# Layer-1 attention: the sum matmuls of a head moved straight behind its last V product, additions of the exponentials in one run, and the orders around them

## The chip, the cores and the metric

The kernel runs as one program on one core of a Trainium2 chip. The metric is the time of one execution on the device in microseconds, the median of several runs. One execution is also taken by the hardware profiler; its rows are counted from the start of the profiled span. The engines are TensorE (PE, with its weight loads PEld), VectorE (DVE), ScalarE (ACT), GpSimd (POOL) and SyncE (SP), which issues the transfers.

## The reference, cut to what matters

Two transformer layers with modulated norms over x of 4 batches x 1024 tokens x 128. The change is inside the attention of the second one (layer 1): 16 heads of width 64 in each of 4 batches, 64 heads in all.

```python
xn = layer_norm(x, ln_gamma, ln_beta)
q, k, v = heads(xn @ Wq), heads(xn @ Wk), heads(xn @ Wv)
att = jnp.einsum('bhid,bhjd->bhij', q, k) / DIM_HEAD ** 0.5
att = att + alibi_bias(S, N_HEADS)[None]
p = jax.nn.softmax(att, axis=-1)
out = jnp.einsum('bhij,bhjd->bhid', p, v)
return out.transpose(0, 2, 1, 3).reshape(B, S, INNER) @ Wo
```

Layer 0 stands before this part, and after it a mixture of experts with a router.

## The kernel before

Each engine has its own program, written out by hand; they meet through counting semaphores. The attention is a loop over pairs of heads; `head(p, s)` is called for the even head (s = 0) and the odd head (s = 1) of pair p, and n = 2p + s. The order of the calls in each engine's `head` is the order in which that engine works.

The scores of a head are 1024 x 1024, kept transposed: 8 tiles j of 128 keys x 1024 queries. In head n TensorE does four things at once, interleaved: the maxima of the next head (`maxima`, 16 matmuls, line 1977), the exact scores of this head (`scores`, 4 matmuls for a tile, lines 1992 and 1993), the V product of this head (`weigh`, 4 instructions for a tile, line 2007, in a run of tiles 0 to 2 and a run of tiles 3 to 7), and the projections of Q and K of head n + 2 (`project_qk`, lines 1943 to 1945, two halves). Even heads also project V (`project_v`, line 1928), odd heads the output of the pair before (`out_proj`, line 2025). V, Q and K, the output projection and the sums all pass through one PSUM bank, number 5.

VectorE reduces the maxima (lines 1031 and 1034), adds the near part of the distance bias to each score tile (`bias`, line 1055), combines the maxima of the two halves by four small operations with both inputs in SBUF (`max_both`, line 1040) and turns them (line 1049), writes the low parts of Q and K (`q_low`, `k_low`, lines 1015 and 1019), inverts the sums in four parts (`invert`, line 1005) and adds the projected output (`add_out`, line 1011). ScalarE takes the exponentials (`exps`, line 1624, one 128 x 1024 tile at a time), copies the sums (`sums`, line 1614), the V product (`outputs`, line 1630), the scaled output in two halves (`turned_out`, line 1636), and makes the high parts of Q and K (lines 1598 and 1601) and their copies (1605 and 1609).

The row sums of the softmax are made in two steps. GpSimd adds the 8 exponentials of a head into one tile, seven additions (`add_head`, lines 646 and 649; each 128 x 1024 float32). TensorE then sums that over its partitions with a matrix of ones (`sum_head`, line 2014, four instructions). GpSimd also multiplies the V product of the head before with the inverted sums (`scaled_out`, line 636), and once per batch it scales the output weights (line 702) and splits the next batch's h in two parts (lines 722 and 725).

Before the change `add_head` for head n does five additions, then `scaled_out` of head n - 1, then the last two. `sum_head` for head n - 1 stands in head n, behind its scores of tile 5 and the maximum (4, 1). ScalarE copies the sums behind the exponential of tile 4, and VectorE's four inversions follow between the maxima (5, 0) and the end of the head:

```python
for j in tiles_:
    if behind and j == T - 2:
        scaled_out(1 - s, n - 1)
```

Waits that matter: `max_half(…, 0, 0)` and the tiles of `scores` wait for Q and K of their head (`q_lo`, `k_lo`, counted in halves); `scores(j)` waits for the exponential of tile j - 2, whose banks it takes; `exps(n, j)` waits for the score, for its bias and for the additions of head n - 1 up to tile j; `scaled_out(n)` waits for the four inversions of head n.

Of the kernel before, what the change touches and what calls it, by code (L numbers as in the profile page):

```python
# [29 lines left out]
T = N // 128  # L30
# [151 lines left out]
def network(nc, a):  # L182
# [7 lines left out]
    with ctx:  # L190
# [405 lines left out]
        def _(pool):  # L596
# [41 lines left out]
            def add_head(s, n, behind=True, tiles_=range(1, T)):  # L638
                for j in tiles_:
                    if behind and j == T - 2:  # L640
                        scaled_out(1 - s, n - 1)
                    k = T * n + j
                    pool.wait_ge(S["exp_done"], k + 1 + EXP_AT)
                    if j == 1:
                        pool.wait_ge(S["sum_mm"], n - 1 + SUM_AT)
                        pool.tensor_tensor(psum8[s][:, :], pfull[:, 0, :], pfull[:, 1, :], ALU.add).then_inc(S["p_added"], 1)
                    else:
                        pool.wait_ge(S["p_added"], (T - 1) * n + j - 1 + ADD_AT)
                        pool.tensor_tensor(psum8[s][:, :], psum8[s][:, :], pfull[:, j % RING, :], ALU.add).then_inc(S["p_added"], 1)  # L649

# [61 lines left out]
            def last_pairs(b):  # L712
# [5 lines left out]
                add_head(1, 2 * p + 1, True, range(1, T - 2))  # L718
                scaled_out(0, 2 * p)
# [6 lines left out]
                add_head(1, 2 * p + 1, False, range(T - 2, T))  # L726
# [15 lines left out]
            add_head(1, HEADS - 1, True, range(1, 4))  # L742
# [40 lines left out]
        def _(dve):  # L783
# [273 lines left out]
            def head(p, s, ahead=2, behind=2):  # L1057
# [12 lines left out]
                maxima((1, 1))  # L1070
                if out:
                    add_out(p - 1, 0)
                maxima((2, 0))
                bias(s, n, 2)
                maxima((2, 1))
                bias(s, n, 3)
                maxima((3, 0), (3, 1))
                bias(s, n, 4)
                if out:
                    add_out(p - 1, 1)  # L1080
                maxima((4, 0))
                bias(s, n, 5)
                maxima((4, 1), (5, 0))
                if behind:
                    invert(o, n - 1, 0)
                maxima((5, 1), (6, 0))
                bias(s, n, 6)
                maxima((6, 1))
                if ahead == 2:
                    q_low(s, n + 2, 0)  # L1090
                    k_low(s, n + 2, 0)
                bias(s, n, 7)
                if behind:
                    invert(o, n - 1, 1)
# [470 lines left out]
        def _(act):  # L1565
# [34 lines left out]
            def k_high(s, n, i, bank=5):  # L1600
                act.activation(half(Ka[s][0:64, :], i), P[64:128, bank, :], ACT.Copy).then_inc(S["k_hi"], 1)
# [36 lines left out]
            def head(p, s, ahead=2, behind=2):  # L1638
                n, o = 2 * p + s, 1 - s
                exps(n, 0)  # L1640
                exps(n, 1)
                if s == 0:
                    values(p, 0)
                if behind == 2:
                    turned_out(s, n - 2, p - 1, 1)
                exps(n, 2)
                exps(n, 3)
# [3 lines left out]
                if behind:  # L1651
                    sums(o, n - 1)
                exps(n, 5)
                if behind:
                    outputs(o, n - 1)
                if ahead == 2:
                    q_high(s, n + 2, 0)
                    k_high(s, n + 2, 0)
                exps(n, 6)
                if ahead:  # L1660
                    k_again(o, n + 1)
                exps(n, 7)
                if ahead == 2:
                    q_high(s, n + 2, 1)
                    k_high(s, n + 2, 1)
                if ahead == 2:
                    q_again(s, n + 2)
                if behind:
                    turned_out(o, n - 1, p - 1 if s == 0 else p, 0)
# [97 lines left out]

            exps(HEADS - 1, 0)
            exps(HEADS - 1, 1)
# [3 lines left out]
            sums(0, HEADS - 2)  # L1773
            exps(HEADS - 1, 5)
            outputs(0, HEADS - 2)
# [75 lines left out]
        def _(pe):  # L1851
# [79 lines left out]
            def project_qk(s, n, i):  # L1931
                if i == 0:
# [95 lines left out]
            def head(p, s, ahead=2, behind=2):  # L2028
# [15 lines left out]
                if out:  # L2044
                    if ahead:
# [10 lines left out]
                if out:  # L2056
                    out_proj(p - 1, 1)
# [4 lines left out]
                maxima((4, 0))  # L2062
                scores(s, n, 5)
                maxima((4, 1))
                if behind:
                    if s == 0:
                        pe.wait_ge(S["v_in"], 2 * p + 2)
                    elif out:
                        pe.wait_ge(S["x_added"], 2 * p + X_AT)
                    else:  # L2070
                        pe.wait_ge(S["q_lo"], 2 * n + 4)
                        pe.wait_ge(S["k_lo"], 2 * n + 4)
                    sum_head(o, n - 1)
                maxima((5, 0))
                scores(s, n, 6)
                maxima((5, 1))
                if ahead == 2:
                    project_qk(s, n + 2, 0)
                maxima((6, 0))
                scores(s, n, 7)  # L2080
                maxima((6, 1))
                weigh(s, n, p, 0)
                weigh(s, n, p, 1)
                weigh(s, n, p, 2)
# [3 lines left out]
                weigh(s, n, p, 3)  # L2088
                weigh(s, n, p, 4)
                weigh(s, n, p, 5)  # L2090
                weigh(s, n, p, 6)
# [406 lines left out]
```

## Time and profile before

| what | value |
|---|---|
| runs | 2318.73, 2315.21, 2315.65 us |
| median | 2315.65 us |
| profiled execution | 2305.89 us |
| its span, first to last instruction | 2304.0 us |
| granted clock, mean over the span | 0.985 |
| PE busy | 2197.2 us, 95% |
| DVE busy | 1829.4 us, 79% |
| POOL busy | 1385.3 us, 60% |
| ACT busy | 1234.0 us, 54% |

The layer-1 attention takes most of the span, from about 440 to about 1940 us. Busy shares are averages over all stages; what holds a stage is read from the stage's own rows. A matmul's time in a row contains the drain of the array, so that in a run of matmuls the distance from start to start is shorter than the time shown.

### The profile page before, as it was taken

To read this page: it belongs to the slowest core of one execution; us is meant where nothing else is said; L and a number is where in the kernel's file an instruction comes from. 1 tells how busy PE (TensorE), PEld (TensorE's weight loads), DVE (VectorE), ACT (ScalarE), POOL (GpSimd) and SP (SyncE) were. 2 spreads that over 40 slices of the span, in tenths; PEclk is the share of its full clock that TensorE was granted. 3 is DMA by queue.
4 is the path that set the end of the run, shared out by engine and by line. 5 is a ranking of instruction groups with operands and counts; after the bars stand their busy time and mean duration, and the time that the engine had idled before them with its cause. 6 is when DMAs were issued, how large, how long until landed. Compare 5 with 4: busy or idle time off the path is not lost. (4 is left out here: it accounts for less than half of the span.)

```text
span 2304.0 us, 40435 instructions
## 1 busy us (share of the span) xinstructions
PE 2197.2 (95%) x10494; PEld 1381.0 (60%) x10531; DVE 1829.4 (79%) x4804; ACT 1234.0 (54%) x1664; POOL 1385.3 (60%) x751
## 2 busy tenths in 40 slices
PE   7989998899999999999999999999999999989995
PEld 4656665456565565656556565655556564449884
DVE  7788886788888888888888888888888887765555
ACT  2232323466666566666656666666666664444442
POOL 2112120578787787878778787887878787643331
PEclk9999999999999999999999999999999999999997
DMA  7050202000000100000100000010000000311114
GB/s 241 22 197 1 85 8 96 21 19 14 16 13 16 35 16 14 13 18 17 34 13 13 21 14 16 13 34 17 14 16 13 20 9 8 148 46 48 46 45 135
DMA packets 90230, 91.25 MB, mean 40 GB/s; under 512 B 22212, under 2 KB 74948, under 8 KB 90120
## 3 DMA queue, kind: packets, MB, share of 16 engines
q1 hardware_dynamic: 85800, 81.35, 11.4%
q0 software_dynamic: 4352, 8.99, 1.2%
q8 instruction: 33, 0.54, 0.1%
q14 instruction: 45, 0.37, 0.1%
HBM read 57.37 MB, written 36.33 MB: 41 GB/s over the span
## 5 line engine op out<-in xcount | busy, mean ns | idle before, releaser
L1624 ACT ACTIVATE big<-P 128x1024 f32<-128x1024 f32 x512 | 512.1, 1020 | 109.2 <-PE P L1993 85.5
L2007 PE MATMUL P<-big,V 128*64 128x512 f32 x2048 | 468.8, 599 | 1.0 <-ACT big L1630 1.0
L649 POOL TENSOR_TENSOR spair<-spair,big 128x1024 f32<-128x1024 f32 x192 | 457.4, 2382 | 15.9 <-DVE hp L810 1.3
L649 POOL TENSOR_TENSOR opair<-opair,big 128x1024 f32<-128x1024 f32 x192 | 457.3, 2382 | 15.0
L1031 DVE CUSTOM_DVE_ANT_0 big<-P,near 128x512 f32<-128x512 f32 x512 | 348.8, 681 | 112.2 <-PE P L1977 108.4
L1977 PE MATMUL P<-kq 96*128 96x512 f32 x1008 | 415.5, 433 | 14.2 <-DVE kq L1015 11.1
L1992 PE MATMUL P<-kq 97*128 97x512 f32 x1024 | 411.4, 402 | 5.7 <-issue 2.8
L1034 DVE TENSOR_REDUCE mhalf<-P 128x1 f32<-128x512 f32 x512 | 349.2, 682 | 79.0 <-PE P L1977 68.5
L1993 PE MATMUL P<-kq 128*128 128x512 f32 x1024 | 408.9, 399 | 0.0
L1977 PEld LDWEIGHTS P<-kq 96*128 96x128 f32 x1008 | 181.8, 190 | 214.3 <-issue 114.0
L2007 PEld LDWEIGHTS P<-big,V 128*64 128x64 f32 x2048 | 135.2, 136 | 265.0 <-issue 262.7
L636 POOL TENSOR_TENSOR big<-big,sinv 128x512 f32<-128x512 f32 x64 | 82.2, 1284 | 309.4 <-DVE sinv L1005 309.4
L1005 DVE RECIPROCAL sinv<-sinv 128x128 f32<-128x128 f32 x256 | 238.0, 931 | 1.9
L1992 PEld LDWEIGHTS P<-kq 97*128 97x128 f32 x1024 | 195.9, 191 | 47.4 <-issue 6.5
L1993 PEld LDWEIGHTS P<-kq 128*128 128x128 f32 x1024 | 196.4, 192 | 45.9
L1636 ACT ACTIVATE big<-big 64x512 f32<-64x512 f32 x128 | 80.8, 631 | 266.4 <-POOL big L636 264.8
L779 POOL DMA_INDIRECT yrows<-xn,tidx x72 | 68.9, 958 | 159.3 <-DVE xn L1531 159.3
L630 POOL TENSOR_TENSOR rstd<-veps,halfneg 128x4 f32<-128x4 f32 x40 | 41.8, 1047 | 199.1 <-DVE veps L803 199.0
L1055 DVE TENSOR_TENSOR P<-P,near 128x128 f32<-128x128 f32 x512 | 149.6, 292 | 7.5 <-PE P L1993 5.6
L1598 ACT ACTIVATE kq<-P 64x512 fp32r<-64x512 f32 x128 | 75.7, 591 | 98.5 <-PE P L1993 88.9
L1830 ACT ACTIVATE hT<-P 128x512 f32<-128x512 f32 x73 | 43.7, 598 | 106.3 <-PE P L2412 106.3
L1710 ACT ACTIVATE big<-P 128x512 f32<-128x512 f32 x72 | 42.6, 597 | 96.2 <-PE P L2101 96.2
(316 smaller groups left out, 3663.1 us busy)
## 6 DMA issues: line engine op xcount, KB each, us to landing
slots<-later SPq DMA_DIRECT2D x4, 4224.0 KB, 15.5
kq<-auxrows SPq DMA_DIRECT2D x64, 128.0 KB, 2.3
big<-in_wex SPq DMA_DIRECT2D x8, 768.0 KB, 11.4
xt<-slots SPq DMA_DIRECT2D x76, 66.0 KB, 1.8
near<-in_aux SPq DMA_DIRECT2D x64, 64.0 KB, 1.8
big<-yrows SPq DMA_DIRECT2D x8, 512.0 KB, 7.2
wqk_hi<-wparts SPq DMA_DIRECT2D x62, 64.0 KB, 1.8
wqk_lo<-wparts SPq DMA_DIRECT2D x62, 64.0 KB, 1.9
```

The costliest lines, as they stand in the source:

```text
L636: pool.tensor_tensor(ohead[s], ohead[s], sinv[s][:, :], ALU.mult).then_inc(S["o_scaled"], 1)
L649: pool.tensor_tensor(psum8[s][:, :], psum8[s][:, :], pfull[:, j % RING, :], ALU.add).then_inc(S["p_added"], 1)
L1005: dve.reciprocal(sinv[s][:, cols], sinv[s][:, cols]).then_inc(S["s_inv"], 1)
L1031: dve.tensor_tensor_reduce(waste, P[:, bank, :], near[s][:, left:left + HALF], -1.0, 3.0e38, ALU.add, ALU.min, mhalf[:, i, t:t + 1]).then_ ...
L1034: dve.tensor_reduce(mhalf[:, i, t:t + 1], P[:, bank, :], AX.X, ALU.max, negate=True).then_inc(S["max_red"], 1)
L1055: dve.tensor_tensor(block, block, near[s][:, ZERO:ZERO + 128], ALU.add).then_inc(S["biased"], 1)
L1624: act.activation(pfull[:, j, :], banks(2 * (j % 2)), ACT.Exp, scale=DH1 ** -0.5).then_inc(S["exp_done"], 1)
L1636: act.activation(half(oT[64 * s:64 * s + 64, :], i), ohead[s][64 * i:64 * i + 64, :], ACT.Copy).then_inc(S["o_norm"], 1)
L1977: pe.matmul(P[:, 6 + i, :], tile(Qa[s][0:MROW, :], t), half(Ka[s][0:MROW, :], i), start=True, stop=True).then_inc(S["max_mm"], 1)
L1992: pe.matmul(P[:, bank + i, :], tile(Ka[s][0:KEXACT, :], j), half(Qa[s][0:KEXACT, :], i), start=True, stop=False)
L1993: mm = pe.matmul(P[:, bank + i, :], tile(Kb[s], j), half(Qb[s], i), start=False, stop=True)
L2007: mm = pe.matmul(P[64 * i:64 * i + 64, 4, :], V1[:, j, s, :], half(pfull[:, j, :], i), start=(j == 0), stop=(j == T - 1))
```

## The change

On GpSimd the additions of a head run from the first to the seventh, and the scaled output of the head before follows behind the last. On TensorE the sums of head n stand at the end of head n, straight behind its last V product, and wait there for Q and K of head n + 2 to have left bank 5; the output projection's two halves stand one maximum later, and in even heads the first half of the Q and K projection stands ahead of the maximum (5, 0). ScalarE copies the sums first thing in the next head, then alternates exponentials and the halves of the turned output, and takes the copy of the V product behind the exponential of tile 2; the first half of K is copied ahead of the first half of Q, with waits of its own. On VectorE the first inversion moves behind the maximum (6, 1), the second behind `max_rows`, and the other two to the head's end; the low part of K's first half comes earlier. The last head of the attention, outside the loop, is reordered alike. The core of the diff:

```diff
             def add_head(s, n, behind=True, tiles_=range(1, T)):
                 for j in tiles_:
-                    if behind and j == T - 2:
-                        scaled_out(1 - s, n - 1)
...
+                if behind:
+                    scaled_out(1 - s, n - 1)
...
                 add_head(0, 2 * p)
-                add_head(1, 2 * p + 1, True, range(1, T - 2))
-                scaled_out(0, 2 * p)
+                add_head(1, 2 * p + 1)
...
-                add_head(1, 2 * p + 1, False, range(T - 2, T))
...
                 bias(s, n, 1)
-                maxima((1, 1))
+                maxima((1, 1), (2, 0))
+                bias(s, n, 2)
+                maxima((2, 1))
                 if out:
                     add_out(p - 1, 0)
-                maxima((2, 0))
-                bias(s, n, 2)
-                maxima((2, 1))
                 bias(s, n, 3)
                 maxima((3, 0), (3, 1))
                 bias(s, n, 4)
+                maxima((4, 0))
                 if out:
                     add_out(p - 1, 1)
-                maxima((4, 0))
                 bias(s, n, 5)
                 maxima((4, 1), (5, 0))
-                if behind:
-                    invert(o, n - 1, 0)
+                bias(s, n, 6)
+                if ahead == 2:
+                    k_low(s, n + 2, 0)
                 maxima((5, 1), (6, 0))
-                bias(s, n, 6)
+                bias(s, n, 7)
                 maxima((6, 1))
                 if ahead == 2:
                     q_low(s, n + 2, 0)
-                    k_low(s, n + 2, 0)
-                bias(s, n, 7)
                 if behind:
-                    invert(o, n - 1, 1)
+                    invert(o, n - 1, 0)
                 maxima((7, 0), (7, 1))
                 if ahead:
                     max_both(n + 1)
                     max_rows(n + 1)
                 if behind:
-                    invert(o, n - 1, 2)
+                    invert(o, n - 1, 1)
                 if ahead == 2:
+                    q_low(s, n + 2, 1)
                     k_low(s, n + 2, 1)
-                    q_low(s, n + 2, 1)
                 if behind:
-                    invert(o, n - 1, 3)
+                    for c in range(2, NINV):
+                        invert(o, n - 1, c)
...
             def k_high(s, n, i, bank=5):
+                if not isinstance(n, int) or n > 1:
+                    act.wait_ge(S["st_mm"], T * (n - 2) + (i + 1) * TPH + ST_AT)
+                act.wait_ge(S["qk_mm"], 2 * n + i + 1)
...
                 n, o = 2 * p + s, 1 - s
+                if behind == 2:
+                    sums(o, n - 1)
                 exps(n, 0)
+                if behind == 2:
+                    turned_out(s, n - 2, p - 1, 0)
                 exps(n, 1)
+                if behind == 2:
+                    turned_out(s, n - 2, p - 1, 1)
                 if s == 0:
                     values(p, 0)
-                if behind == 2:
-                    turned_out(s, n - 2, p - 1, 1)
                 exps(n, 2)
+                if behind:
+                    outputs(o, n - 1)
                 exps(n, 3)
...
-                if behind:
-                    turned_out(o, n - 1, p - 1 if s == 0 else p, 0)
...
+                        pe.wait_ge(S["s_copied"], 2 * p)
...
                         pe.wait_ge(S["h_part_ok"], n)
-                    if not isinstance(n, int) or n > 2:
-                        pe.wait_ge(S["s_copied"], n - 2)
-                    elif n == 2:
-                        pe.wait_ge(S["v_in"], 2)
+                        pe.wait_ge(S["v_in"], n)
+                    elif isinstance(n, int) and n == 3:
+                        pe.wait_ge(S["s_copied"], 1)
+                    else:
+                        pe.wait_ge(S["x_added"], n - 3 + X_AT)
...
-                if out:
-                    if ahead:
-                        pe.wait_ge(S["q_lo"], 2 * n + 4)
-                        pe.wait_ge(S["k_lo"], 2 * n + 4)
-                    else:
-                        pe.wait_ge(S["s_copied"], n - 1)
-                    out_proj(p - 1, 0)
                 maxima((2, 0))
                 scores(s, n, 2)
                 maxima((2, 1))
+                if out:
+                    pe.wait_ge(S["s_copied"], n)
+                    out_proj(p - 1, 0)
                 scores(s, n, 3)
...
                 maxima((4, 0))
+                if out:
+                    out_proj(p - 1, 1)
...
                 scores(s, n, 5)
                 maxima((4, 1))
-                if behind:
...
-                    sum_head(o, n - 1)
+                if s == 0 and ahead == 2:
+                    project_qk(s, n + 2, 0)
                 maxima((5, 0))
+                if s == 1 and ahead == 2:
+                    project_qk(s, n + 2, 0)
                 scores(s, n, 6)
...
+                for j in range(3, T):
+                    weigh(s, n, p, j)
+                if ahead == 2:
+                    pe.wait_ge(S["q_lo"], 2 * n + 6)
+                    pe.wait_ge(S["k_lo"], 2 * n + 6)
+                else:
+                    pe.wait_ge(S["v_in"], 2 * p + 2)
+                sum_head(s, n)
```

## Rows read from the trace of the kernel before

**Rows 1.** The page: busy time by engine, and one of the costliest groups.

```profile
PE 2197.2 (95%) x10494; PEld 1381.0 (60%) x10531; DVE 1829.4 (79%) x4804; ACT 1234.0 (54%) x1664; POOL 1385.3 (60%) x751
...
L1636 ACT ACTIVATE big<-big 64x512 f32<-64x512 f32 x128 | 80.8, 631 | 266.4 <-POOL big L636 264.8
```

**Rows 2.** Windows, one head each: us; busy PE, PEld, DVE, ACT, POOL; clock, DMA.

```profile
1000.65:1024.06 23.41, 23.41 (x109) 14.03 (x107) 20.35 (x47) 14.57 (x18) 17.86 (x9) 1.00 0.03 9
760.43:787.56 27.13, 25.05 (x106) 15.28 (x106) 22.58 (x47) 14.68 (x18) 22.41 (x10) 0.94 0.06 21
1140.72:1167.39 26.67, 24.79 (x106) 15.25 (x107) 22.27 (x47) 14.69 (x18) 22.33 (x10) 0.94 0.05 20
1520.76:1546.10 25.34, 23.50 (x106) 14.00 (x106) 21.92 (x47) 14.58 (x18) 21.00 (x10) 1.00 0.06 18
```

**Rows 3.** Timeline of PE in one odd head: start us, us, instruction, count.

```profile
1012.88 0.73 PE L1977 MATMUL P<-kq 96*128 96x512 f32 x2
...
1022.73 0.39 PE L1977 MATMUL P<-kq 96*128 96x512 f32 x1
1023.05 1.08 PE L2014 MATMUL P<-opair,ones 128*64 128x512 f32 x4
1024.06 0.50 PE L1977 MATMUL P<-kq 96*128 96x512 f32 x1
1024.40 0.40 PE L1992 MATMUL P<-kq 97*128 97x512 f32 x1
...
1027.76 2.79 PE L2007 MATMUL P<-big,V 128*64 128x512 f32 x12
1030.48 0.73 PE L1977 MATMUL P<-kq 96*128 96x512 f32 x2
...
1031.85 4.51 PE L2007 MATMUL P<-big,V 128*64 128x512 f32 x20
```

**Rows 4.** Timeline of POOL in the same head.

```profile
1022.03 9.75 POOL L649 TENSOR_TENSOR spair<-spair,big 128x1024 f32<-128x1024 f32 x4
1036.91 1.28 POOL L636 TENSOR_TENSOR big<-big,sinv 128x512 f32<-128x512 f32 x1 [5.14 <-DVE sinv L1005]
```

**Rows 5.** Timelines of DVE and ACT in the same head.

```profile
1014.97 0.29 DVE L1055 TENSOR_TENSOR P<-P,near 128x128 f32<-128x128 f32 x1
...
1021.43 0.29 DVE L1055 TENSOR_TENSOR P<-P,near 128x128 f32<-128x128 f32 x1
...
1021.87 1.03 ACT L1624 ACTIVATE big<-P 128x1024 f32<-128x1024 f32 x1 [0.99 <-PE P L1993]
```

**Rows 6.** DVE's L1040 in the same head, and over the attention by tile.

```profile
1032.53 0.74 DVE L1040 TENSOR_TENSOR mneg<-mhalf 32x8 fp32r<-32x8 f32 x4
...
L1040 DVE TENSOR_TENSOR mneg<-mhalf x252: 159/163/2272, 438.8 to 1908.5; 32x8 fp32r<-32x8 f32 x126
```

**Rows 7.** Timelines of POOL and DVE in three other heads.

```profile
765.38 7.41 POOL L649 TENSOR_TENSOR opair<-opair,big 128x1024 f32<-128x1024 f32 x3
...
864.10 4.82 POOL L649 TENSOR_TENSOR opair<-opair,big 128x1024 f32<-128x1024 f32 x2
867.30 2.23 DVE L1040 TENSOR_TENSOR mneg<-mhalf 32x8 fp32r<-32x8 f32 x4
...
1143.09 9.76 POOL L649 TENSOR_TENSOR opair<-opair,big 128x1024 f32<-128x1024 f32 x4
1150.20 2.87 DVE L1040 TENSOR_TENSOR mneg<-mhalf 32x8 fp32r<-32x8 f32 x4
```

**Rows 8.** Waits of the attention (total, times, longest), and PE's timeline behind two.

```profile
PE P L1977 <- DVE kq L1015: 11.1, 7, 2.1
...
775.84 0.73 PE L1977 MATMUL P<-kq 96*128 96x512 f32 x2 [2.08 <-DVE kq L1015]
...
1155.91 0.72 PE L1977 MATMUL P<-kq 96*128 96x512 f32 x2 [1.87 <-DVE kq L1015]
```

**Rows 9.** Window behind the second of these waits.

```profile
1156.52:1159.93 3.41, 3.41 (x10) 2.65 (x9) 2.60 (x8) 1.65 (x2) 3.21 (x2) 0.50 0.00 0
```

More of the change, by code:

```diff
@@ L741, in _ @@
             add_head(0, HEADS - 2)
-            add_head(1, HEADS - 1, True, range(1, 4))
+            add_head(1, HEADS - 1, False, range(1, 4))
             inverse_root("d0")
@@ L1650, in head @@
                 exps(n, 4)
-                if behind:
+                if behind == 1:
                     sums(o, n - 1)
                 exps(n, 5)
-                if behind:
-                    outputs(o, n - 1)
+                if ahead == 2:
+                    k_high(s, n + 2, 0)
+                exps(n, 6)
                 if ahead == 2:
                     q_high(s, n + 2, 0)
-                    k_high(s, n + 2, 0)
-                exps(n, 6)
-                if ahead:
-                    k_again(o, n + 1)
                 exps(n, 7)
@@ L1665, in head @@
                     k_high(s, n + 2, 1)
+                if ahead:
+                    k_again(o, n + 1)
                 if ahead == 2:
                     q_again(s, n + 2)
-                if behind:
-                    turned_out(o, n - 1, p - 1 if s == 0 else p, 0)
             act.sem_inc(S["exp_done"], EXP_AT)
@@ L1766, in route_exp @@
                 act.activation(rexp[:, :, 0:E1], rlog[:, :, 0:E1], ACT.Exp).then_inc(S["rd_exp"], 1)
+            sums(0, HEADS - 2)
             exps(HEADS - 1, 0)
+            turned_out(1, HEADS - 3, ALL_PAIRS - 2, 0)
             exps(HEADS - 1, 1)
@@ L1772, in _ @@
                 exps(HEADS - 1, j)
-            sums(0, HEADS - 2)
+            outputs(0, HEADS - 2)
             exps(HEADS - 1, 5)
-            outputs(0, HEADS - 2)
             exps(HEADS - 1, 6)
@@ L2043, in head @@
                     project_v(p, 0)
-                if out:
-                    if ahead:
-                        pe.wait_ge(S["q_lo"], 2 * n + 4)
-                        pe.wait_ge(S["k_lo"], 2 * n + 4)
-                    else:
-                        pe.wait_ge(S["s_copied"], n - 1)
-                    out_proj(p - 1, 0)
                 maxima((2, 0))
@@ L2053, in head @@
                 maxima((2, 1))
+                if out:
+                    pe.wait_ge(S["s_copied"], n)
+                    out_proj(p - 1, 0)
                 scores(s, n, 3)
                 maxima((3, 0))
-                if out:
-                    out_proj(p - 1, 1)
                 if s == 0:
@@ L2062, in head @@
                 maxima((4, 0))
+                if out:
+                    out_proj(p - 1, 1)
+                if behind == 1:
+                    pe.wait_ge(S["q_lo"], 2 * n + 4)
+                    pe.wait_ge(S["k_lo"], 2 * n + 4)
+                    sum_head(o, n - 1)
                 scores(s, n, 5)
                 maxima((4, 1))
[L2065 to L2072, printed above, removed]
-                    sum_head(o, n - 1)
+                if s == 0 and ahead == 2:
+                    project_qk(s, n + 2, 0)
                 maxima((5, 0))
+                if s == 1 and ahead == 2:
+                    project_qk(s, n + 2, 0)
                 scores(s, n, 6)
[L2076 to L2079, printed above, removed]
+                maxima((5, 1), (6, 0))
                 scores(s, n, 7)
                 maxima((6, 1))
-                weigh(s, n, p, 0)
-                weigh(s, n, p, 1)
-                weigh(s, n, p, 2)
+                for j in range(3):
+                    weigh(s, n, p, j)
                 maxima((7, 0), (7, 1))
@@ L2087, in head @@
                     project_qk(s, n + 2, 1)
[L2088 to L2091, printed above, removed]
-                weigh(s, n, p, 7)
+                for j in range(3, T):
+                    weigh(s, n, p, j)
+                if ahead == 2:
+                    pe.wait_ge(S["q_lo"], 2 * n + 6)
[3 more added lines that the diff above has]
+                sum_head(s, n)
             pe.sem_inc(S["st_mm"], ST_AT)
@@ L2326, in _ @@
             scores(1, HEADS - 1, 1)
-            pe.wait_ge(S["s_copied"], HEADS - 2)
+            pe.wait_ge(S["s_copied"], HEADS - 1)
             out_proj(ALL_PAIRS - 2, 0)
@@ L2333, in _ @@
             scores(1, HEADS - 1, 5)
-            pe.wait_ge(S["x_added"], 2 * (ALL_PAIRS - 1) + X_AT)
-            sum_head(0, HEADS - 2)
             scores(1, HEADS - 1, 6)
```

## The prediction

> **What bounds the kernel now.** I read the page first, then the stretches, then the engines' timelines over one head. TensorE is busy 95% of the span [rows 1], so the reader should look for where it is not back to back. Layer-1 attention is 64 heads, and in the steady part a head takes 23.41 us with TensorE busy all of it [rows 2]. Of the other engines GpSimd is the next to look at: it is busy 17.9 of these 23.4 us [rows 2], nearly all with seven additions, and its timeline shows where most of the rest lies: 5.1 us in one piece, between the fifth addition of a head and the product with the inverted sums [rows 4]. Times below that stand without a row number are counted from a head's start, the issue of its first maximum matmul (1012.88 in the head shown).
>
> Some stretches of the loop are longer, three of them by 1.9 to 3.7 us [rows 2]. Seven times in the attention TensorE waits for VectorE's L1015, 11.1 us in all [rows 8], and behind each the reader finds the same thing: an L1040 operation that takes 0.16 us in the median and up to 2.27 us [rows 6]. That is what decides this change, so I come back to it.
>
> **The gain on TensorE.** Today the four sum matmuls stand alone among the score matmuls. From the maximum before them (1022.73) to the score behind them (1024.40) go 1.67 us [rows 3]. Two neighbouring matmuls of that kind take 0.235 us each in plain sequence, and four matmuls of the V form cost (4.51 - 2.79) / 8 x 4 = 0.86 us inside a run [rows 3]. So 1.67 - 0.47 - 0.86 = 0.34 us is what the switch in and out costs, and it falls away when the sums follow the last V product. V itself is in runs of 12 and 20 instructions before and after, so nothing there. 62 heads x 0.34 = 21 us, if TensorE stays the bound.
>
> **What the moves on ScalarE, VectorE and SP do.** The number of operations is unchanged on every engine; only order and waits differ. The first bias of a head ends at 2.38 (1014.97 + 0.29), and an exponential starts 0.15 us after its bias when ScalarE is free (1021.72 to 1021.87) [rows 5]. The first exponential therefore runs from 2.53 to 3.55. Now the first half of the turned output (0.63 us, rows of L1636 [rows 1]) stands between it and the second, which ends at 5.2 rather than 4.6. The output projection no longer stands ahead of scores(2) in odd heads, so that score waits for the first exponential: some 0.3 us of the gain go back there. The earlier copies of the K halves, the added waits on s_copied, v_in and x_added and the sums copied first on ScalarE are released before their turn by this count, and I cost them at nothing; the cover is that ScalarE is idle a third of the head [rows 2]. SP issues the same transfers, released no later than their use.
>
> **GpSimd without the stop.** The first addition needs the second exponential, so it starts at 5.3. Four in a row take 9.75 us [rows 4] and two take 4.82 [rows 7], so each further one is 2.46 and seven take 9.75 + 3 x 2.46 = 17.1. They end at 22.4, the sixth from 17.6 to 20.0, the seventh from 20.0 to 22.4. The product with the inverted sums follows after the last inversion, at the start of the next head, ahead of need. On GpSimd alone the sums could start at 22.5, about where TensorE arrives. So far this is 23.2 to 23.5 us a head, next to no change.
>
> **The wait that takes the place.** At the end of a head's maxima VectorE issues L1040 four times: two inputs in SBUF, 32x8, 0.74 us for the four when GpSimd is idle [rows 6]. In the kernel before they fall just into GpSimd's 5.1 us pause (1032.53, pause 1031.78 to 1036.91). In nine heads, where GpSimd is late, they do not, and then they wait for the addition under way. One: additions from 1143.09 end at 1152.85; the four from 1150.20 end at 1153.07. Another: additions end at 868.92, the four end at 869.53 [rows 7]. In all nine, the blocked operation ends 0.02 to 0.04 us after the addition. In three of these the first was blocked by the last addition but one; two of the four slipped through the gap between additions and the third was blocked again until the last one ended.
>
> In the changed order they start 1.9 to 2.05 us after the maxima (7, 0) are issued (1030.48 to 1032.53 [rows 3, 6]). Those were issued at 17.6; without the sum run and with the small stalls above they come at 16.3 to 16.9, so L1040 starts at 18.2 to 18.9. That is inside the sixth addition in every head. Two pass at 20.0, the third waits to 22.4. What is queued behind on VectorE: the transpose, an inversion, q_low and k_low, and for those two the sum matmuls wait by their new wait on bank 5. Today's example measures that chain: additions end at 1152.85, TensorE resumes at 1155.91 [rows 7, 8], 3.06 us. So the sums start at 22.4 + 3.06 = 25.5, their run takes 1.01 (1023.05 to 1024.06 [rows 3]), and the head is 26.5 us long instead of 23.42: **+3.05 us a head, x 62 = +189 us**. The longer head does not dissolve it, since the additions and L1040 are both counted from the same head start.
>
> Of that exclusion the reverse is in doubt. In the row with two L1040 in the gap, four additions take 9.76 us against 9.75 without [rows 4, 7]: GpSimd loses nothing. The Trainium skill (SBUF — State Buffer, section Who interferes with whom) says that a VectorE instruction with two SBUF inputs and a GpSimd instruction that reads SBUF share one interface, and the one that issues first holds it for the whole instruction while the other fully blocks. By that the additions too would lose up to 2 x 0.16 us a head, an estimate of 20 us more in the sum. By the row they lose nothing, and I go by the row.
>
> **The clock.** TensorE then stands still for 2.8 to 3 us before each sum. After the waits of 2.08 and 1.87 us in the kernel before the granted clock was 0.50, the 1.2 GHz level, for 3.41 us [rows 8, 9]; the third such head kept 1.00 [rows 2]. These stretches lost 27.13 - 23.42 - 2.08 = 1.6 and 26.67 - 23.42 - 1.87 = 1.4 us. In the new head much of such a stretch has slack, since the additions set the end; what counts is the delay of the second exponential, 0.3 to 0.7, and of L1040. I take 0.7 us in two heads of three, 0.45 a head, **+28 us**; bounds 0 and 1.5 a head (0 to 93 us).
>
> **One-off terms.** The seven waits (11.1), the lowered clock (3.0) and three waits for additions (some 1.5) of before are contained in the new head length: **-16 us**. In some 14 heads, outside GpSimd's inner loops, three additions take 7.41 us [rows 7] where 2.36 + 2 x 2.46 = 7.28 would do, 0.06 a step and 0.4 us over seven; and splitting the next batch's h (some 3.6 us on GpSimd, three times) pushes the first addition by about 0.5: together **+7 us**.
>
> **The sum.** 189 + 28 - 16 + 7 = +208 us. The profiled execution took 2305.89 us (span 2304.0, 1.9 around it), so its changed twin should take about 2514. The median of the runs is 2315.65, 9.8 above the profiled one; I carry that over: **2524 us**, 9% slower.
>
> **The rivals.**
> *No blocking worth the name* (the nine heads had another cause, or L1040 falls clear). Then TensorE with its 0.34 us gain, the 0.3 us stall and the additions ending at 22.4 hold each other at 23.2 to 23.5 us a head: 62 x (-0.2 to +0.1) - 16 + 7 gives 2294 to 2313, most likely 2303, faster. For it speaks that TensorE is the bound today and that 237 of the 252 L1040 ran freely; against it that these ran while GpSimd stood still. It decides if L1040 starts later than 22.4 or before the fifth addition ends (17.5). Chance 0.06.
> *One addition only.* All four pass in the gap at 20.0. Then q_low and k_low are through at about 23.1, the head is 24.2 us: 62 x 0.8 - 9 = +41, 2357 us. Against it: in three of three cases only two passed. Chance 0.07.
> *The clock falls in every head at the old price.* 62 x (3.05 + 1.5) - 9 = +273, 2589 us. For it: the stall is longer than the two that lowered the clock. Against it: a slow stretch brings TensorE later to the sums, so the next stall is shorter. Chance 0.07.
>
> **How the numbers follow.** The forecast case has 0.80. Its own bounds: a second exponential at 4.9 instead of 5.2 and no clock loss, 62 x 2.75 - 9 = +161, 2477; clock loss nearly everywhere, +1.4 a head, +265, 2580. Range 2470 to 2585, which leaves the three rivals out. Differences under 0.2% (4.6 us) can't be told from no change here. Faster 0.04, same 0.02 (both from the first rival, whose upper end lies within that bound), slower 0.94.
>
> **What would show it.** In the changed profile: sums straight behind the V run with a wait of 2 to 3 us ahead of them, released by VectorE's L1015 or L1019; L1040 with a mean of about 1 us instead of 0.16, its end 0.2 us behind the seventh addition; seven additions without a pause and GpSimd idle only from there to the next head's second exponential; head to head 26 to 27.5 us; granted clock at 0.50 in many stretches. I am wrong if L1040 stays at 0.16 us, if the sums wait for L649 instead, or if heads stay below 24 us.

## The result and the profile after

The changed kernel takes 2538.81 us in the median of four runs (2536.25 to 2544.91), beside 2315.43 in the median of four for the kernel before: ratio 1.0967, 95% interval 1.0942 to 1.0993. The forecast was 2524 us, in a range of 2470 to 2585. The profiled run took 2544.91 us. One run of after_filled3, an experiment below, took 8175.40 us, and nothing that was kept says why; its numbers are those of its three other runs.

The page after: busy time by engine, the chain that ended last by engine and line, and the group of the minimum of the maxima (L1040 before, L1038 now).

```profile
PE 2287.9 (90%) x10494; PEld 1429.5 (56%) x10531; DVE 1991.8 (78%) x4804; ACT 1245.5 (49%) x1664; POOL 1389.5 (55%) x751
...
PE 66%; DVE 19%; issue 9%; POOL 2%; ACT 1%; DMA 1%; DVEq 1%; another core or an unknown queue 0%; POOLq 0%; SPq 0%; ACTq 0%
...
L1038 DVE TENSOR_TENSOR mneg<-mhalf 32x8 fp32r<-32x8 f32 x256 | 223.9, 874 | 8.2
```

TensorE's share fell from 95% to 90% [rows 1], VectorE stands in the chain with 19%, and the minimum's mean is 0.87 us. Its row by tile (shortest, median, longest in ns) says how that mean is made, and the waits of the attention who pays (total, times, longest):

```profile
L1038 DVE TENSOR_TENSOR mneg<-mhalf x256: 159/167/2299, 397.9 to 2132.0; 32x8 fp32r<-32x8 f32 x128
```
```profile
PE P L2020 <- DVE kq L1017: 147.4, 61, 3.5
```

Half of these operations, called pieces from here on, run at 0.16 us, and the others take up to 2.3. Behind each head's V products TensorE now waits for the low part of K: 61 times, 2.4 us in the mean, where [rows 8] had seven such waits. One head on all engines (timelines; start us, us, instruction, count):

```profile
1101.74 0.63 ACT L1636 ACTIVATE big<-big 64x512 f32<-64x512 f32 x1
1102.40 1.02 ACT L1624 ACTIVATE big<-P 128x1024 f32<-128x1024 f32 x1
```
```profile
1103.58 2.40 POOL L644 TENSOR_TENSOR spair<-big 128x1024 f32<-128x1024 f32 x1 [3.51 <-ACT big L1624]
1106.07 14.67 POOL L647 TENSOR_TENSOR spair<-spair,big 128x1024 f32<-128x1024 f32 x6
```
```profile
1117.04 3.91 DVE L1038 TENSOR_TENSOR mneg<-mhalf 32x8 fp32r<-32x8 f32 x4
1121.18 0.20 DVE L1047 STREAM_TRANSPOSE mrows<-mneg 32x32 f32<-32x32 f32 x1 [0.23 <-DVE mneg L1038]
1121.32 0.90 DVE L1003 RECIPROCAL sinv<-sinv 128x128 f32<-128x128 f32 x1
1122.15 0.61 DVE L1013 TENSOR_TENSOR kq<-P,kq 64x512 fp32r<-64x512 f32 x1
1122.79 0.69 DVE L1017 TENSOR_TENSOR kq<-P,kq 64x512 fp32r<-64x512 f32 x1
```
```profile
1116.54 4.51 PE L2013 MATMUL P<-big,V 128*64 128x512 f32 x20
1123.73 1.08 PE L2020 MATMUL P<-spair,ones 128*64 128x512 f32 x4 [2.68 <-DVE kq L1017]
1124.74 0.73 PE L1983 MATMUL P<-kq 96*128 96x512 f32 x2
```

Read it from the back: the sums at 1123.73 wait for the subtraction that ends at 1123.48; before it in VectorE's order stand another, an inversion and the transpose, which waits for the minimum; and the minimum, four operations worth 0.74 us [rows 6], lasts from 1117.04 to 1120.95 because the six additions run to 1120.74: its first piece takes 1.26 us and ends 0.03 us behind the sixth addition of the head, its third takes 2.24 and ends 0.02 behind the seventh. The V products, by contrast, were issued out at about 1121.

The windows (columns as in [rows 2]) show this head, the next, one with a lowered clock, and the start of that one:

```profile
1097.15:1123.73 26.58, 23.85 (x106) 13.96 (x107) 23.43 (x48) 14.93 (x18) 17.97 (x8) 1.00 0.03 8
1123.73:1149.98 26.25, 23.59 (x106) 14.11 (x107) 22.27 (x46) 15.54 (x20) 17.95 (x8) 1.00 0.08 20
1068.91:1097.15 28.24, 26.21 (x107) 15.77 (x107) 21.78 (x46) 15.80 (x20) 17.98 (x8) 0.89 0.07 19
1068.40:1075.23 6.83, 6.32 (x14) 3.78 (x15) 4.41 (x10) 1.84 (x3) 1.28 (x1) 0.50 0.13 38
```

The kernel before has 23.41 us here. From the sums at 494.56 us to those at 2106.60 lie 59 heads, 27.3 us each. Twenty of them, with a granted clock of 0.99 or 1.00, take 26.2 to 26.6 us: nearly all the even ones 26.3, the odd ones 26.6.

### The profile page after: what moved, and what is told of

Its sections match the earlier page's. It is cut to its first block, busy times and chain, and to the rows that moved or that the text cites. A ratio compares the mean times of both kernels' runs of the same rounds, so it can differ in the third digit from the quotient of the medians.

```text
span 2543.1 us, 40649 instructions
## 1 busy us (share of the span) xinstructions
PE 2287.9 (90%) x10494; PEld 1429.5 (56%) x10531; DVE 1991.8 (78%) x4804; ACT 1245.5 (49%) x1664; POOL 1389.5 (55%) x751
## 4 chain that ended last, share of the span: by engine, by line
PE 66%; DVE 19%; issue 9%; POOL 2%; ACT 1%; DMA 1%; DVEq 1%; another core or an unknown queue 0%; POOLq 0%; SPq 0%; ACTq 0%
PE P L1983 11%; PE P L1998 9%; PE P L1999 8%; PE P L2013 7%; DVE mneg L1038 6%; PE P L2020 4%; PE P L2420 3%; PE P L2115 3%; PE P L2031 2%; PE P L1933 2%; PE P L2101 2%; DVE big L1029 2%; DVE kq L1017 2%; DVE kq L1013 2%; PE P L2391 1%
## 5 line engine op out<-in xcount | busy, mean ns | idle before, releaser
L1624 ACT ACTIVATE big<-P 128x1024 f32<-128x1024 f32 x512 | 525.0, 1026 | 259.4 <-DVE P L1053 131.6
L647 POOL TENSOR_TENSOR opair<-opair,big 128x1024 f32<-128x1024 f32 x192 | 457.0, 2380 | 18.9 <-ACT big L1624 1.9
L647 POOL TENSOR_TENSOR spair<-spair,big 128x1024 f32<-128x1024 f32 x192 | 456.8, 2379 | 18.9 <-DVE hp L808 1.3
L1998 PE MATMUL P<-kq 97*128 97x512 f32 x1024 | 437.5, 427 | 6.2 <-issue 3.7
L1999 PE MATMUL P<-kq 128*128 128x512 f32 x1024 | 424.0, 414 | 0.0
L1983 PE MATMUL P<-kq 96*128 96x512 f32 x1008 | 406.9, 450 | 6.3 <-DVE kq L1017 1.4
L1983 PEld LDWEIGHTS P<-kq 96*128 96x128 f32 x1008 | 192.6, 202 | 208.1 <-issue 129.8
L1998 PEld LDWEIGHTS P<-kq 97*128 97x128 f32 x1024 | 210.3, 205 | 61.5 <-ACT big L1624 8.2
L1999 PEld LDWEIGHTS P<-kq 128*128 128x128 f32 x1024 | 209.5, 205 | 46.6
L1038 DVE TENSOR_TENSOR mneg<-mhalf 32x8 fp32r<-32x8 f32 x256 | 223.9, 874 | 8.2
L1614 ACT ACTIVATE sinv<-P 128x512 f32<-128x512 f32 x64 | 38.2, 597 | 324.8 <-PE P L2020 324.8
L644 POOL TENSOR_TENSOR spair<-big 128x1024 f32<-128x1024 f32 x32 | 76.6, 2395 | 137.9 <-ACT big L1624 131.4
```

Of the source, the lines that this page charges most:

```text
L1038: dve.tensor_tensor(mneg[:, b::4], mhalf[rows, 0, :], mhalf[rows, 1, :], ALU.min).then_inc(S["max_both"], 1)
L1624: act.activation(pfull[:, j, :], banks(2 * (j % 2)), ACT.Exp, scale=DH1 ** -0.5).then_inc(S["exp_done"], 1)
L1983: pe.matmul(P[:, 6 + i, :], tile(Qa[s][0:MROW, :], t), half(Ka[s][0:MROW, :], i), start=True, stop=True).then_inc(S["max_mm"], 1)
L1998: pe.matmul(P[:, bank + i, :], tile(Ka[s][0:KEXACT, :], j), half(Qa[s][0:KEXACT, :], i), start=True, stop=False)
L1999: mm = pe.matmul(P[:, bank + i, :], tile(Kb[s], j), half(Qb[s], i), start=False, stop=True)
```

## The experiments

The kernel before was run again beside each group of experiments, with medians of 2312.56 to 2317.10 us, so that their times can be set against each other.

**One operand instead of two.** The minimum of two arrays became a reduction of one, in the changed kernel and in the kernel before; it is as long (0.74 us for four).

```
-dve.tensor_tensor(mneg[:, b::4], mhalf[rows, 0, :], mhalf[rows, 1, :], ALU.min)
+dve.tensor_reduce(mneg[:, b::4], mhalf[rows, :, :].rearrange("p i t -> p t i"), AX.X, ALU.min)
```

> The changed kernel with one line different: the four operations that combine the maxima of the two halves (128 columns of keys by 8, two inputs in SBUF) become reductions over one input. Theory (GpSimd's additions shut out a VectorE operation with two inputs in SBUF): the four take about 0.75 us again whatever GpSimd does, the wait of 1.9 to 2.8 us ahead of the sums falls away, a head takes 23.2 to 23.5 us instead of 27.3, the granted clock stays at 1.00 through the attention, and the time is 2285 to 2315 us. Rival (the moved sums and their wait on bank 5 cost the time whatever the kind of operation): a head stays above 26 us, the time at 2500 us or more. Rival (VectorE is late because it does more before its q_low and k_low): the four are short, but the sums still wait 1 us or more, 2380 us or more.

> The kernel before with the same one line different. Theory: the seven waits of 1.2 to 2.1 us for VectorE and the two stretches of lowered clock behind them go, 13 to 16 us less: about 2300 us (ratio 0.993 to 0.995). Rival (those seven heads are late because GpSimd is late with its own results): the waits stay, 2315 us, ratio 1.00.

after_reduce: 2311.15 us, ratio 0.9983 (0.9968 to 0.9997). before_reduce: 2302.37 us, ratio 0.9948 (0.9928 to 0.9968). In after_reduce, timelines of GpSimd, VectorE and TensorE:

```profile
1109.10 14.64 POOL L647 TENSOR_TENSOR spair<-spair,big 128x1024 f32<-128x1024 f32 x6
```
```profile
1120.08 0.74 DVE L1038 TENSOR_REDUCE mneg<-mhalf 32x8 fp32r<-32x16 f32 x4
```
```profile
1123.92 1.03 PE L2020 MATMUL P<-spair,ones 128*64 128x512 f32 x4
```

The additions are the same six in the same time, the minimum runs in the middle of them at its old price, and the wait for the low part of K ahead of the sums is gone. This line takes 228 us from the changed kernel's time, where the change had added 223, so the rest of the change is not what made it slow. In the kernel before it also removes the seven waits of [rows 8] and gains 14 us. The Trainium skill (SBUF — State Buffer, section Who interferes with whom) says that a VectorE instruction with at most one SBUF input, outside the two-port modes, does not contend with GpSimd, and that a reduction on trn2 never does; the trace agrees, 0.16 or 0.17 us a piece in all 256.

**Work in the old pause.** The kernel before, with one more GpSimd instruction between the fifth addition and the scaling, another one in each of three runs. It fills a row of the buffer that nobody uses then.

```
 if behind and j == T - 2:
+    pool.tensor_tensor(big[:, 3, :], pfull[:, T - 4, :], pfull[:, T - 3, :], ALU.add)  # before_reads
+    pool.memset(big[:, 3, :], 0.0)                                                      # before_writes
+    pool.memset(<the same row as 128 x 2048 of two bytes>, 0.0)                         # before_writes3
     scaled_out(1 - s, n - 1)
```

> The kernel before with one more GpSimd addition (two exponential tiles, 128 x 1024, into a part of SBUF that nobody reads) in its pause ahead of the scaled output, in every head that has one. The result is not touched. Theory: the combining operations start at 1032.53 in the shown head, inside the new addition (about 1031.85 to 1034.2), and end 1.6 us later than before; 0.3 us of that is slack, so a head gets 1.2 to 1.4 us longer: 2315 + 62 x 1.3 = 2395 us, more if the clock falls too. Rival (an addition in GpSimd's pause is idle time filled): 2315 to 2320 us.

> As the run with one more addition, but the GpSimd operation put into the pause only writes (a memset of the same 128 x 1024 part of SBUF). By the Trainium skill (SBUF — State Buffer, section Who interferes with whom) a VectorE instruction with two SBUF inputs contends with a GpSimd instruction that reads SBUF and not with one that only writes: the combining operations stay at 0.16 us, 2315 us. If any GpSimd operation shuts them out: they end with the memset, and a head gets longer by what the memset reaches beyond 1033.6 in the shown head, which can be seen in its row.

> The kernel before with a long write without a read on GpSimd in the pause (the unused row of the buffer, in 2048 elements of two bytes; the earlier one lasted 0.94 us and met the minimum for 0.14 us only). Theory A (only instructions that read both of their operands there shut VectorE out): the minimum's four pieces run at 0.16 us each while the write runs, 2318 to 2325 us. Rival B (any GpSimd instruction does): the pieces end with the write or pass two in a gap, and heads become up to 1.5 us longer, 2340 to 2410 us.

Each was run once. before_reads took 2413.47 us (before: 2316.46). The additional addition with the scaling behind it, the minimum, and TensorE's wait in the attention:

```profile
1018.69 2.36 POOL L641 TENSOR_TENSOR big<-big 128x1024 f32<-128x1024 f32 x1
1025.31 1.29 POOL L636 TENSOR_TENSOR big<-big,sinv 128x512 f32<-128x512 f32 x1 [4.25 <-DVE sinv L1006]
```
```profile
1019.30 2.37 DVE L1041 TENSOR_TENSOR mneg<-mhalf 32x8 fp32r<-32x8 f32 x4
```
```profile
PE P L1978 <- DVE kq L1016: 82.1, 50, 4.2
```

The pause was long enough for the addition: GpSimd still waits 4.25 us for VectorE's inversion behind it, so GpSimd itself is not late. What it does to the minimum costs 97 us. Most heads take 24.8 to 24.9 us, 1.4 more than before; ten with a granted clock of 0.88 to 0.94 take 26.4 to 29.9. before_writes took 2318.61 us, but its write of 0.94 us met the minimum for only 0.14 us and decides nothing. before_writes3 took 2319.22 us (before: 2317.1), with a write that covers the minimum:

```profile
1051.52 2.43 POOL L641 MEMSET big<- 128x2048 bf16 x1
```
```profile
1052.37 0.75 DVE L1041 TENSOR_TENSOR mneg<-mhalf 32x8 fp32r<-32x8 f32 x4
```

A GpSimd instruction that reads two operands from SBUF shuts the minimum out, one that only writes does not. The same section of the Trainium skill makes this distinction, for any GpSimd instruction that reads SBUF; one with a single operand from SBUF was not run.

**The missing stop alone.** The kernel before with the scaling behind the seventh addition, and nothing else of the change.

```
-if behind and j == T - 2:
-    scaled_out(1 - s, n - 1)
 ...
+if behind and T - 2 in tiles_:      # behind the loop over the additions
+    scaled_out(1 - s, n - 1)
```

> The kernel before with one part of the change alone: the multiplication by the inverted sums stands behind a head's seventh addition instead of between the fifth and the sixth, so that the additions run without a stop; the sums, V's products and every other order are those of before. Theory (the missing stop alone brings the loss): the minimum of the maxima has no pause to fall in, two of its pieces end with the seventh addition in every head (mean of a piece about 0.9 us instead of 0.16), TensorE waits some 2 to 3 us for the low half of K ahead of the next head's maxima, heads of 26 to 27 us, 2470 to 2560 us. Rival (it takes the sums behind V, whose wait stands ahead of everything else on TensorE): at most the second piece is late, 2316 to 2400 us.

One run: 2478.02 us (before: 2312.56). Timelines of GpSimd, VectorE and TensorE in one head:

```profile
999.75 14.67 POOL L647 TENSOR_TENSOR opair<-opair,big 128x1024 f32<-128x1024 f32 x6
```
```profile
1011.92 2.91 DVE L1040 TENSOR_TENSOR mneg<-mhalf 32x8 fp32r<-32x8 f32 x4
```
```profile
1017.66 0.73 PE L1977 MATMUL P<-kq 96*128 96x512 f32 x2 [1.91 <-DVE kq L1015]
```

The minimum ends 0.41 us behind the last addition (1014.42), and the wait is there, now ahead of the next head's maxima. In nearly every head only one of the four pieces is long, so that their mean is 0.67 us where I expected about 0.9. This one part brings 165 us by itself, of the 223 of the whole change; the sums need not be moved for it. Two neighbouring heads (columns as in [rows 2]):

```profile
1082.90:1108.27 25.37, 23.51 (x108) 14.04 (x107) 21.53 (x46) 15.54 (x20) 17.79 (x9) 1.00 0.07 21
1108.27:1134.95 26.68, 24.80 (x108) 15.19 (x107) 22.58 (x47) 14.68 (x18) 18.16 (x9) 0.94 0.02 8
```

The waits are alike in both (1.8 to 2.1 us over the attention). Where the granted clock stays at 1.00 a head takes about 25.3 us, 1.9 more than before; where it is 0.94, in 40 of 60 heads, it takes 26.6 to 27.0. So some 60 of the 165 us are the clock's, an estimate from 40 heads at 1.5 us. What makes the other 58 of the 223 us no run shows by itself. In the changed kernel the sums (1.01 us) stand in the chain behind the minimum, and half of the turned output (0.63 us) ahead of the second exponential.

**A stop put back.** The changed kernel, with GpSimd waiting for the minimum ahead of the seventh addition.

```
+if j == T - 1 and (not isinstance(n, int) or 1 < n < HEADS - 1):
+    pool.wait_ge(S["max_both"], 4 * n + 8)
 pool.wait_ge(S["p_added"], (T - 1) * n + j - 1 + ADD_AT)
```

> The changed kernel with one wait more: GpSimd does not start the seventh addition of a head before VectorE's minimum of the maxima is written. Theory (the minimum is shut out by the additions, and the chain behind its end sets the head): the pieces all pass behind the sixth addition and end at about 21.75 us after the sums of the head before instead of 23.45, the seventh addition starts 0.8 us later, and the sums come 2.9 us behind the pieces: heads of 24.6 to 24.9 us instead of 26.25 at the full clock, 2400 to 2440 us, though GpSimd does the same work with a stop in it. Rival (the additions are the bound and the minimum is only slow beside them): GpSimd ends 0.8 us later, heads are 0.8 us longer, 2580 to 2600 us.

2365.87 us, ratio 1.0206 (1.0183 to 1.0228), below the range expected: a wait more, and the changed kernel is 173 us faster. GpSimd, VectorE and TensorE in one head:

```profile
1060.50 12.22 POOL L649 TENSOR_TENSOR opair<-opair,big 128x1024 f32<-128x1024 f32 x5
1073.49 2.36 POOL L649 TENSOR_TENSOR opair<-opair,big 128x1024 f32<-128x1024 f32 x1 [0.77 <-DVE mneg L1040]
```
```profile
1071.57 1.76 DVE L1040 TENSOR_TENSOR mneg<-mhalf 32x8 fp32r<-32x8 f32 x4
```
```profile
1076.11 1.08 PE L2022 MATMUL P<-opair,ones 128*64 128x512 f32 x4 [0.53 <-DVE kq L1019]
```

The pieces end at 1073.33, 0.6 us behind the sixth addition, and the sums start 2.78 us later, the same 2.78 us as in the changed kernel (1120.95 to 1123.73). Heads are 24.2 and 24.5 us. So the head's length follows the end of the minimum, not that of the additions: the seventh starts 0.77 us behind the sixth, as it waits for the minimum, and still ends 0.26 us ahead of the sums (1075.85). The heads are 0.4 us shorter than expected, and the granted clock is 0.987 in the mean of the run instead of 0.947, which makes the time lower than I had said.

**The wait filled.** The changed kernel with products that nobody reads between the last V product and the wait, so that TensorE does not stand still.

```
 if ahead == 2:
+    for _ in range(3):              # after_filled: 5
+        for i in range(NHALF):
+            pe.matmul(P[64 * i:64 * i + 64, 0, :], ones[:, :], half(pfull[:, T - 1, :], i), start=True, stop=True)
     pe.wait_ge(S["q_lo"], 2 * n + 6)
```

> The changed kernel with five pairs of products more between the last V product and the wait ahead of the sums, into a bank that is free then and that nobody reads (2.1 us of TensorE at full clock, in a wait of 2.6 us). Theory (the heads above 26.6 us are the clock's, which falls after the waits ahead of the sums): with the wait filled the clock stays up, the heads are 26.3 to 26.6 us throughout instead of 27.3 in the mean, 2480 to 2500 us. Rival (the clock falls for another reason, or the longer heads are other waits): 2530 to 2550 us, the stretches at half clock remain; if TensorE is the bound rather than the chain, 2600 us and more.

> As after_filled, with three pairs of products instead of five: a product of this shape takes TensorE two passes of 0.43 us a pair, so that five pairs took 4.3 us and outlasted the wait; three take 2.56 us and end before it (2.9 us from the last V product to the sums). Theory (the sums still come 2.8 us behind the minimum, so that the filling costs nothing, and the clock that no longer falls gives back what the heads above 26.6 us lost): heads of 26.2 to 26.6 us throughout, no stretch at half clock in the attention, 2480 to 2500 us. Rival (the longer heads of the changed kernel have another cause): 2530 to 2550 us as the changed kernel.

after_filled: 2575.37 us, ratio 1.1111 (1.1091 to 1.113). I had counted a pair as one pass; it takes two, and the 4.3 us outlasted the wait, so TensorE itself became the bound at 27.7 and 28.0 us a head. That does not decide between the two theories, though the granted clock was 1.00 in all these heads. after_filled3: 2492.26 us (2491.88 to 2494.44), ratio 1.0757 (1.0736 to 1.0779). Its TensorE ahead of one head's sums, and the windows of two heads and of the attention:

```profile
1127.64 2.74 PE L2090 MATMUL P<-big,ones 128*64 128x512 f32 x12
1130.40 1.08 PE L2020 MATMUL P<-opair,ones 128*64 128x512 f32 x4
```
```profile
1104.14:1130.40 26.26, 26.12 (x119) 14.97 (x119) 22.30 (x46) 15.52 (x20) 17.95 (x8) 1.00 0.07 20
1130.40:1157.00 26.60, 26.45 (x119) 14.85 (x119) 23.43 (x48) 14.93 (x18) 17.96 (x8) 1.00 0.02 8
445.00:2060.00 1615.00, 1602.08 (x7184) 906.72 (x7183) 1397.68 (x2802) 927.54 (x1157) 1113.67 (x498) 1.00 0.06 16
```

The heads now have the length of the changed kernel's full-clock heads, and the clock is 1.00 throughout. Useless work makes the changed kernel 2538.81 - 2492.26 = 47 us faster: that is the clock's share of the loss, and the chain behind the minimum has the rest.

**The gain that was left.** after_reduce has no blocked minimum, yet it is not as fast as before_reduce. Its heads are 23.43 us (even) and 23.70 (odd) against 23.42. TensorE in an odd head, at the third scores and at the seventh tile's first maximum:

```profile
1056.93 0.66 PE L1983 MATMUL P<-kq 96*128 96x512 f32 x2
1057.64 0.50 PE L1998 MATMUL P<-kq 97*128 97x512 f32 x1
1057.98 0.40 PE L1999 MATMUL P<-kq 128*128 128x512 f32 x1
...
1067.53 0.39 PE L1999 MATMUL P<-kq 128*128 128x512 f32 x1
1067.90 0.50 PE L1983 MATMUL P<-kq 96*128 96x512 f32 x1
1068.33 2.79 PE L2013 MATMUL P<-big,V 128*64 128x512 f32 x12
```

The matmuls follow each other at 0.235 us, save at 1057.64, where 0.36 us are lost over two steps (the first exponential ends there), and at 1067.90 and 1068.33 (0.13 and 0.2; the bank has just been freed by VectorE's maximum, which stands behind the low part of K). I put both down to VectorE's order, so two neighbours were swapped in it, on top of after_reduce:

```
-maxima((0, 0), (0, 1))
+maxima((0, 0))
 bias(s, n, 0)
-maxima((1, 0))
+maxima((0, 1), (1, 0))
 ...
+maxima((5, 1))
 k_low(s, n + 2, 0)          # if ahead == 2
-maxima((5, 1), (6, 0))
+maxima((6, 0))
```

> The changed kernel with the reduction of one operand in place of the minimum of two (as in after_reduce, 2311), and two neighbours swapped in VectorE's order: the first addition to the scores ahead of the second maximum, and the low half of K behind the sixth tile's first maximum instead of ahead of it. Theory (the sums behind V do give TensorE 0.3 us a head, and what after_reduce loses again are two stalls that its trace shows: 0.36 us ahead of the third scores of odd heads, which wait for the first exponential, and about 0.3 us ahead of the seventh tile's first maximum in all heads, which waits for VectorE): heads of 23.1 to 23.2 us, 2280 to 2295 us, below before_reduce (2302). Rival (the stalls only move on to the next wait, or GpSimd's seven additions, which then end just ahead of the sums, set the head): heads as in after_reduce, 23.43 and 23.70, 2308 to 2314 us.

2284.8 us, ratio 0.9855 (0.9839 to 0.9872), the fastest of all and below both kernels. Two heads, and TensorE at the same two places of the second, which is odd:

```profile
1018.75:1041.89 23.14, 23.14 (x109) 14.20 (x107) 19.28 (x46) 15.66 (x20) 18.01 (x8) 1.00 0.08 21
1041.89:1065.05 23.16, 23.16 (x108) 14.04 (x106) 20.23 (x48) 15.04 (x18) 17.95 (x8) 1.00 0.04 11
```
```profile
1045.75 0.66 PE L1984 MATMUL P<-kq 96*128 96x512 f32 x2
1046.25 0.39 PE L1999 MATMUL P<-kq 97*128 97x512 f32 x1
...
1056.02 0.39 PE L2000 MATMUL P<-kq 128*128 128x512 f32 x1
1056.25 0.44 PE L1984 MATMUL P<-kq 96*128 96x512 f32 x1
1056.62 2.80 PE L2014 MATMUL P<-big,V 128*64 128x512 f32 x12
```

The third scores now start 0.50 us behind the maxima instead of 0.71, and the seventh tile's maximum 0.23 us behind the scores instead of 0.37. The step into the V product is still 0.37 us, so that of its 0.2 us only 0.06 were VectorE's. TensorE is busy all of both heads, and they are 0.27 us shorter than before_reduce's 23.42. The sums behind V do pay, once nothing waits for them.

## Why the prediction was right, and where a size was off

The time lay 15 us above the forecast, and the mechanism is the one forecast: the clock cost 19 us more than it was given, and the rest 4 us less. With the times counted as there (head start 1098.16 in the head shown, where the sums' run ends):

- **The additions without a stop.** Second exponential done at 5.26 (forecast 5.2), first addition at 5.42 (5.3), last addition done at 22.58 (22.4).
- **The minimum.** It starts at 18.88 (18.2 to 18.9), inside the sixth addition; its end is 0.21 us behind the seventh. The runs on one operand, on reading and on writing show that this is exclusion by GpSimd's reads and not another wait, and before_nostop that the missing stop is what sets it free to happen.
- **The chain behind it.** 2.99 us from the last addition to the sums (3.06), sums at 25.57 (25.5), head 26.25 to 26.6 (26.5). In after_filled3, with the clock out of the way, the loss against the kernel before on its chip is 2492.26 - 2316.74 = 176 us; the forecast without its clock term is 189 - 16 + 7 = 180.
- **What additions lose.** Nothing, as I had taken from [rows 4, 7]: the six take 14.67 us here and 14.64 in after_reduce, where no operation with two SBUF inputs meets them. The other reading, that a small VectorE instruction holds them up, would have cost 0.3 us a head.
- **The clock, mis-sized.** I took 28 us, as 0.7 us in two heads of three; it is 47. The share of heads was right (39 of 59 are longer than 26.7 us). The step that failed is the price, which set the delay of the second exponential at 0.3 to 0.7 us. In the slow head from 1068.91, an even one, it ends 7.78 us after the start of the sums (first row below); in the even head from 1123.73, at the full clock, 5.97 (second row). That is 1.8 us, and as the additions, the minimum and the chain follow from it without slack, and the additions take 0.2 us more here, the head is 2.0 us longer (28.24 against 26.25). Over the 39 longer heads the second exponential is 1.2 us later in the mean and the head 1.4 us longer than the full-clock heads of the same parity. 47 us over two thirds of 62 heads are 1.1 us in each, where I had 0.7; the bound of 1.5 us a head in the mean held, though single heads lose more.

```profile
1075.67 1.02 ACT L1624 ACTIVATE big<-P 128x1024 f32<-128x1024 f32 x1
...
1128.69 1.01 ACT L1624 ACTIVATE big<-P 128x1024 f32<-128x1024 f32 x1
```

- **TensorE's gain.** Forecast 0.34 us a head from the switch in and out; after_order shows 0.27 over before_reduce, with the change's other moves on TensorE in it. The stall of odd heads, forecast at 0.3 us, is 0.36 in after_reduce.
- **The rivals.** No blocking: after_reduce is that case made by hand, and its 2311 lies in the 2294 to 2313 worked out for it, above its likeliest 2303, because a second stall (the seventh tile's maximum) had not been seen. One addition only: no, in the head shown the third piece ends with the seventh addition and the fourth behind it, and 125 of the 252 pieces are long, two in nearly every head. A slow clock in every head: no, 39 of the 59 heads are longer than 26.7 us, the other 20 are not.
- **One-off terms.** The -16 us for the waits of before: before_reduce, which removes the seven waits and the lowered clock behind them, gains 14.
- **Slips in the working.** In the kernel before 240 of the 252 pieces ran freely, not 237. The upper bound, 62 x (3.05 + 1.4) - 9, is 267, not 265. TensorE stands still for 1.9 to 2.9 us before the sums (once 3.5), 2.4 in the mean, where I had 2.8 to 3. None of the three changes the argument.

## What to carry to other kernels

Before a pause of one engine is closed, list what the other engines do in it: here the 5 us in which GpSimd seemed to lose time were the place in a head where a VectorE operation on two SBUF operands could run unhindered. Count the operation that might be shut out from the same origin as the work that shuts it out, and follow what is queued behind it; and where there is a form with one operand from SBUF at the same price, take that form before moving anything. A TensorE wait of 2 to 3 us can cost more than itself: here the granted clock was 0.50 behind many of them, and the work that then restarts stands at the head of the chain that sets the next wait.

## What the runs showed that was not expected

Two results stand nowhere in the prediction. Products which nobody reads, put into a wait, make the kernel 47 us faster: the granted clock is 1.00 over 1615 us of attention, where the changed kernel has 0.50 in 40 stretches, 195 us in all, with waits of 2.4 us in the mean. And one more wait on GpSimd, which holds the seventh addition back by 0.77 us a head, takes 2.1 us off the head (24.2 and 24.5 against 26.3 and 26.6 at the full clock).
